# Splitting the score maxima on VectorE, and reading the hidden layer's banks together, in a fused attention block

## The reference, cut to what matters

```python
q = rope(x @ Wq.T + bq) * HEAD_DIM ** -0.5      # 16 heads of 16
k = rope(x @ Wk.T + bk)
v = x @ Wv.T + bv
attn = softmax(q @ k.T)                          # 1024 x 1024 a head
x = layernorm(x + (attn @ v) @ Wo.T + bo)
W1q, W2q = ternary(W1), ternary(W2)              # each weight -1, 0 or 1
h = relu(x @ W1q.T + b1)                         # 1024 hidden features
x = layernorm(x + h @ W2q.T + b2)
```

## Time and profile before

| | |
|---|---|
| median of 3 runs | 3485.83 us (3482.68 to 3487.73) |
| the profiled execution | 3487.73 us, span 3485.9 us |
| mean granted TensorE clock | 0.969 of full |
| PE busy | 3324.2 us, 95% |
| PE weight loads busy | 1817.4 us, 52% |
| DVE busy | 2981.4 us, 86% |
| ACT busy | 2513.1 us, 72% |
| POOL busy | 2110.0 us, 61% |

### The profile page before, as it was taken

The page is one execution under the profiler, slowest core; times in us unless marked ns, Lnnn a source line. Parts: engine busy times, 40 slices in busy tenths (PEclk is TensorE's granted clock), DMA queues, the critical chain, the costliest instruction groups (busy, mean ns, idle before and its releaser), DMA issues.

```text
span 3485.9 us, 80529 instructions
## 1 busy us (share of the span) xinstructions
PE 3324.2 (95%) x30726; PEld 1817.4 (52%) x30726; DVE 2981.4 (86%) x5543; ACT 2513.1 (72%) x4884; POOL 2110.0 (61%) x2281
## 2 busy tenths in 40 slices
PE   4898999999999999999999999999999999999975
PEld 3443455555555555555555555555555555544444
DVE  4777899999999999999999999999999999999611
ACT  2156777777777777777777777777777777777740
POOL 2133576677666766676667666766676667643446
PEclk9589999999999999999999999999999999999987
DMA  5334344544453345344543454345434544444110
GB/s 144 49 81 96 90 96 112 111 101 93 112 119 95 91 112 119 95 93 110 119 100 90 110 118 101 98 103 115 104 100 99 114 102 104 96 91 82 34 41 25
DMA packets 292290, 336.94 MB, mean 97 GB/s; under 512 B 59712, under 2 KB 241856, under 8 KB 291648
## 3 DMA queue, kind: packets, MB, share of 16 engines
q1 hardware_dynamic: 291904, 331.79, 41.4%
HBM read 193.27 MB, written 138.41 MB: 95 GB/s over the span
## 4 chain that ended last, share of the span: by engine, by line
PE 92%; POOL 2%; DVE 2%; ACT 1%; DMA 1%; issue 1%; SPq 0%; POOLq 0%; DVEq 0%; ACTq 0%
PE ob L652 29%; PE sc L635 28%; PE job L507 25%; PE ms L624 9%; DVE mxp L1027 1%; ACT prob L756 1%; POOL hid_r L1100 1%; PE job L560 0%; PE ms L507 0%; POOL ka L1186 0%; PE ob L507 0%; DMA qa<-qk_parts 0%; DMA xt_sb<-xt 0%; DVE mxp L879 0%; DMA maxima<-nm 0%
## 5 line engine op out<-in xcount | busy, mean ns | idle before, releaser
L879 DVE TENSOR_REDUCE mxp<-ms 128x1 f32<-128x512 f32 x4032 | 2602.6, 683 | 276.0 <-PE ms L624 226.6
L756 ACT ACTIVATE prob<-sc 128x512 f32<-128x512 f32 x4096 | 2225.4, 597 | 743.0 <-PE sc L635 717.3
L635 PE MATMUL sc<-qa,ka 50*128 50x512 f32 x4096 | 1556.4, 446 | 41.9 <-ACT prob L756 35.0
L624 PE MATMUL ms<-ka,qa 48*128 48x512 f32 x4032 | 1540.8, 449 | 2.0 <-DVE mxp L879 2.0
L635 PEld LDWEIGHTS sc<-qa,ka 50*128 50x128 f32 x4096 | 688.3, 186 | 1142.5 <-ACT prob L756 1023.6
L652 PE MATMUL ob<-prob,v_sb 128*17 128x512 f32 x8192 | 1087.4, 603 | 0.3
L624 PEld LDWEIGHTS ms<-ka,qa 48*128 48x128 f32 x4032 | 681.4, 186 | 16.6 <-DVE mxp L879 13.9
L1079 POOL TENSOR_TENSOR ve<-mv,eps_sb 128x2 f32<-128x2 f32 x128 | 24.9, 194 | 576.2 <-DVE mv L906 576.2
L1100 POOL TENSOR_TENSOR hid_r<-hid,hid_r 128x512 fp32r<-128x512 f32 x256 | 328.8, 1284 | 20.5
L1068 POOL TENSOR_TENSOR xt_r<-xt_sb,xt_r 128x512 fp32r<-128x512 f32 x64 | 83.3, 1301 | 328.6 <-ACT xt_r L768 302.9
L507 PEld LDWEIGHTS job<-h_t,w_sb 64*128 64x128 f32 x3840 | 261.5, 186 | 22.8
(11 more groups left out here) (101 smaller groups left out, 2768.0 us busy)
## 6 DMA issues: line engine op xcount, KB each, us to landing
qk_parts<-parts SPq DMA_DIRECT2D x128, 512.0 KB, 4.7
ka<-qk_parts SPq DMA_DIRECT2D x384, 128.0 KB, 4.5
qa<-qk_parts SPq DMA_DIRECT2D x384, 128.0 KB, 7.4
attention<-at_st SPq DMA_DIRECT2D x128, 256.0 KB, 2.9
v_ones<-v_st SPq DMA_DIRECT2D x64, 272.0 KB, 3.3
v_sb<-v_ones SPq DMA_DIRECT2D x64, 272.0 KB, 8.7
xt_sb<-xt SPq DMA_DIRECT2D x64, 256.0 KB, 4.8
xn<-x SPq DMA_DIRECT2D x64, 256.0 KB, 4.6
```

The lines of the kernel that those rows point to most:

```text
L624: nc.tensor.matmul(ms[upto(b, g, NS1, at) % MS_BANKS][:, :], operand(qa, b, g, j, ROWS)[:, qt * P:(qt + 1) * P], operand(ka, b, g, j, ROWS ...
L635: nc.tensor.matmul(sc[upto(b, g, HG * STEPS, n) % SC_BANKS][:, :], operand(ka, b, g, j, ROWS + MROWS)[:, tt * P:(tt + 1) * P], operand(qa, ...
L756: nc.scalar.activation(prob[st_ % 2][:, j, :], sc[upto(b, g, HG * STEPS, n) % SC_BANKS][:, :], ACT.Exp).then_inc(s["exp_done"], 1)
L879: nc.vector.reduce_max(mxp[(b * G + g) % 2][:, kh, j * TT + qt:j * TT + qt + 1], ms[upto(b, g, NS1, at) % MS_BANKS][:, :], AX.X).then_inc( ...
```

## The change

There are two parts.

**Maxima.** The table `MAXIMA_AT` gets `turn` in part 1 of step 8 instead of part 2, and two new entries, `high` in part 2 and `low` in part 3. Both are DVE instructions on 128x32 elements: `high` multiplies the transposed maxima by -1 and writes the high part (one input in SBUF), `low` multiplies by -1 and subtracts the high part (two inputs in SBUF). POOL's `split_maxima`, three instructions a unit, is gone, with its tiles `neg` and `zeros` and the semaphore `negated`.

**Hidden tiles.** At `f1` and `f3` ACT takes both tiles of `job[0]` between exponentials 1 and 2, and `finish_rest` is gone. DVE takes both tiles of `job[1]` in part 1, instead of one in part 1 and one in part 2.

```diff
-MAXIMA_AT = {(8, 0): "combine", (8, 2): "turn"}
+MAXIMA_AT = {(8, 0): "combine", (8, 1): "turn", (8, 2): "high", (8, 3): "low"}
...
                 elif name in ("f1", "f3"):
-                    take_hidden(b, g, int(name[1]) - 1, job[0][:, 0:TQ])
-
-            def finish_rest(job_):
-                stage, at, name = job_
-                if name in ("f1", "f3"):
-                    take_hidden(*at, int(name[1]), job[0][:, TQ:2 * TQ])
+                    for p in range(2):
+                        take_hidden(b, g, int(name[1]) - 1 + p, job[0][:, p * TQ:(p + 1) * TQ])
...
                         exps(b, g, st_, 3)
-                        for job_ in jobs_at(b, g, st_, tail):
-                            finish_rest(job_)
...
+                elif part == "high":
+                    dve.wait_ge(s["mx_turned"], upto(b, g, 1, 1))
+                    wait_used(dve, s["m_stored"], upto(b, g, 32, 0))
+                    nc.vector.tensor_scalar(nm[:, 0, :], mxt[:, :], -1.0, None, ALU.mult).then_inc(s["high_done"], 1)
+                elif part == "low":
+                    dve.wait_ge(s["high_done"], upto(b, g, 1, 1))
+                    nc.vector.scalar_tensor_tensor(out=nm[:, 1, :], in0=mxt[:, :], scalar=-1.0, in1=nm[:, 0, :],
+                                                   op0=ALU.mult, op1=ALU.subtract).then_inc(s["mx_taken"], 1)
...
-                            for stage, at, name in jobs_at(b, g, st_, tail):
-                                if stage == "proj" and part == 1:
+                            for stage, at, name in jobs_at(b, g, st_, tail) if part == 1 else []:
+                                if stage == "proj":
                                     take_key_half(*at, name)
-                                elif name in ("f1", "f3") and part in (1, 2):
-                                    p = part - 1
-                                    take_hidden(*at, int(name[1]) - 1 + p, job[1][:, p * TQ:(p + 1) * TQ])
+                                elif name in ("f1", "f3"):
+                                    for p in range(2):
+                                        take_hidden(*at, int(name[1]) - 1 + p, job[1][:, p * TQ:(p + 1) * TQ])
...
-            def split_maxima(b, g):
-
-                pool.wait_ge(s["mx_turned"], upto(b, g, 1, 1))
-                nc.gpsimd.tensor_tensor(neg[:, :], zeros[:, :], mxt[:, :], ALU.subtract).then_inc(s["negated"], 1)
-                pool.wait_ge(s["negated"], upto(b, g, 1, 1))
-                wait_used(pool, s["m_stored"], upto(b, g, 32, 0))
-                nc.gpsimd.tensor_copy(nm[:, 0, :], neg[:, :]).then_inc(s["high_done"], 1)
-                pool.wait_ge(s["high_done"], upto(b, g, 1, 1))
-                nc.gpsimd.tensor_tensor(nm[:, 1, :], neg[:, :], nm[:, 0, :], ALU.subtract).then_inc(s["mx_taken"], 1)
...
-                if not (last and g == G - 1):
-                    split_maxima(b + (g + 1) // G, (g + 1) % G)
...
-            split_maxima(0, 0)
```

More of the change, by code:

```diff
@@ L192, in build @@
         eps_sb = sb("eps_sb", [P, TL])
-        zeros = sb("zeros", [P, HG * TT])
         asum = sb("asum", [P, 2])
@@ L216, in build @@
         mxt = sb("mxt", [P, HG * TT])
-        neg = sb("neg", [P, HG * TT])
         nm = sb("nm", [P, MROWS, HG * TT], fp32r)
@@ L258, in build @@
             rotated parts_done parts_stored v_stored
-            m_stored m_loaded s1_ready s1_taken max_done mx_turned negated high_done mx_taken
+            m_stored m_loaded s1_ready s1_taken max_done mx_turned high_done mx_taken
             s2_ready exp_done pv_done o_taken ob_zero
@@ L1136, in finish_second_norm, with unit @@
                                         ).then_inc(s["res_done"], 1)
-            def unit(b, g, tail, tail_before, last):
+            def unit(b, g, tail, tail_before):
                 proj = projected(b, g)
@@ L1174, in unit, with batch @@
                     normalise(*prepared(b, g))
-            def batch(b, tail=True, tail_before=True, last=False):
+            def batch(b, tail=True, tail_before=True):
                 for g in range(G):
-                    unit(b, g, tail, tail_before, last)
+                    unit(b, g, tail, tail_before)
             nc.gpsimd.memset(half_sb[:, :], -0.5).then_inc(s["powers_set"], 1)
             nc.gpsimd.memset(eps_sb[:, :], EPS).then_inc(s["powers_set"], 1)
-            nc.gpsimd.memset(zeros[:, :], 0.0).then_inc(s["powers_set"], 1)
-            pool.wait_ge(s["powers_set"], 3)
+            pool.wait_ge(s["powers_set"], 2)
             for i in range(2 * RING):
@@ L1200, in _ @@
             batch(B - 2)
-            batch(B - 1, last=True)
+            batch(B - 1)
             finish_second_norm(B - 2, G - 1)
```

## The result

The changed kernel took 3530.85 us (median of 4 runs, 3526.58 to 3533.51); the kernel before took 3485.2 beside it. The ratio is 1.013, interval [1.0112, 1.0147]: 45.6 us slower, where I had forecast 56 (3541). The profiled execution took 3532.56, its span 3530.8.

The account below looks back on a forecast made before the run. The loop closing each step, through ACT's exponentials, and PE's almost equally late matmul stream were taken as the bound. -14.5 + 22 + 50 = +57.5, less 2 for overlap, +56, gave 3541 us; range 3484 to 3578.

Parts of the forecast that it names:

- The start: First two units: inputs issued earlier, ACT's stalls of 5.9 and 5.1 us go, plus 3.5 for PE's clock: -14.5 us.
- Hidden tiles on ACT: Second tile ahead of exponentials 2 and 3 delays the next step's second score: 0.37 us in 60 units, 22 us.
- Maxima on DVE: `high` and `low` wait for POOL: 0.75 in step 9, 0.3 in step 10, minus 0.13; 54 units, 50 us.
- The lock that doesn't bite: Rival: `high` and `low` are short enough to get in between POOL's instructions; sum +7, 3493 us; chance 0.18.
- six: Sign: `low` takes at most 0.3 us in the last six units with a tail, where POOL is idle.
- POOL not let go between its instructions: Rival: `high` too waits for POOL's second instruction, third and fourth pair of step 9 stall; 3575 us; chance 0.11.
- The faster side: Rival: PE has room for the late second score in steps 10 and 12, no lock wait; 3477 us; chance 0.08.
- The start that keeps its stalls: Rival: something else holds the inputs at the start, such as POOL's split parts; 3556 us; chance 0.05.
- ACT's copies: Sign the forecast is right: ACT's input copies at the end of the first two units wait for nothing.

Follow-up runs that it names:

- pool_early: The kernel before with POOL's split of the maxima moved ahead of the second set's rotations, in the first two units alone: 3474.99 us against 3487.91, ratio 0.9965.
- hidden_only: The kernel before with the hidden tiles grouped on both ACT and DVE, the maxima staying on POOL: 3511.45 us against 3487.91, ratio 1.0065.
- hidden_dve_only: The kernel before with the hidden tiles grouped on DVE alone, ACT keeping its order: 3491.61 us against 3487.91, ratio 1.0005.
- act_late: The changed kernel with ACT's order of before (second hidden tile after exponential 3), DVE's tiles still grouped: 3519.13 us against 3489.8, ratio 1.0079.
- after_halves: The changed kernel with each of POOL's four sums cut into two instructions of half the length: 3502.36 us against 3488.26 for the kernel before, ratio 1.004.
- low_zero: The changed kernel with the low part written as zeros by a DVE instruction that reads nothing: 3502.01 us against 3489.8 for the kernel before, ratio 1.0034.

## Why the prediction was right

The direction and the mechanisms were right, the sum 10 us too high.

*The start (-14.5).* Right. The stalls that end are 5.9 in the first unit, 7.2 in the second and 1.4 in the third, slow clock included: 14.5. `pool_early`, which touches only them, gained 12.9 [6.3, 18.1 by its ratio's interval]. The clock in the windows from 200 to 290 us, before and after:

```profile
200.00:290.00 90.00, 76.96 (x602) 35.34 (x598) 64.89 (x109) 58.59 (x114) 42.29 (x36) 0.91 0.40 93
```

```profile
200.00:290.00 90.00, 85.61 (x716) 39.58 (x715) 77.58 (x136) 68.55 (x134) 50.25 (x37) 1.00 0.48 105
```

After a wait of PE it stood at 1.2 GHz before; without these waits it stays at 2.4.

*Hidden tiles on ACT (+22).* Right: `hidden_only` has 0.405 us a unit for my 0.37, 24 us over 60 units, and `hidden_dve_only` shows that nothing of it is DVE's while the maxima stay on POOL.

*Maxima on DVE (+50).* Right in kind, too large in size, and this is the step that was mis-sized: 0.75 + 0.3 - 0.13 = 0.92 a unit, where the changed kernel has 1.131 - 0.405 = 0.73 (39 us). Step 10 came as forecast, 3.40. Step 9 grew by 0.57, not 0.75. I had let `low` begin its own work at POOL's recorded end and so put step 9's first reduction 1.79 into the step; it starts at 1.64 (1708.94), since `low` ends at 1709.01, only 0.05 after line 328's record (1708.96), and not its own length of 0.18 after it. Over 54 units the 0.19 between 0.92 and 0.73 is 10 us, as much as the whole miss. The other terms differ less: with -14.5, +24 and +39 the sum is 49, inside the interval of the result (39 to 51). Step 10's cause I had right too (the third reduction, 0.5 into the step for my 0.6); `act_late` shows that the ACT part isn't added to it there, so to take off 0.13 was right.

*The rivals.* The lock that doesn't bite (3493) is out: `low` takes 0.75 in all 54 units with the sums there and 0.18 to 0.19 in the last five (five, where I had written six: the last unit makes no maxima), and `after_halves` and `low_zero` each bring step 9 back to 3.18. POOL not let go between its instructions (3575) is out: `high` ends at 1707.75, while line 328's record has begun at 1707.66, and a reduction runs behind it. The faster side (3477) is out with `hidden_only`: 0.405 is above its point of 0.24 a unit. The start that keeps its stalls (3556) is out by ACT's copies.

Two inputs aren't needed for the wait. The Trainium skill (SBUF — State Buffer, "SBUF: two separate sides") names instructions with two SBUF inputs and those in a 2-port mode. `high` has one input, and it waits in every steady unit (0.66 us at least); the transpose, also with one input, takes its 0.20 beside POOL. That agrees with the page if `high` runs in such a mode, which no run here shows.

## What to carry to other kernels

A short DVE instruction on SBUF of the kind of `high` or `low` costs what is left of POOL's current instruction, so its price is read from what POOL does at that place, not from its own length. Shorter POOL instructions made it cheap here (`low` 0.19 instead of 0.75). Two changes that are tried alone can hide a cost that they have together: DVE's grouped tiles cost 0.006 us a unit alone and 0.161 behind the maxima. Before a small step is moved from one engine to another, ask which queue it delayed in its old place: here the waits in SP's queue in the first two units were all there was to gain, and reordering it alone gave 0.5%. A read of PSUM placed ahead of two exponentials delays the bank that the next step's second score waits for; here two such reads a unit, 0.37 us each, came out as 0.4 a unit.

## What the hardware showed that I had not expected

- `high` and `low` end 0.03 to 0.05 us after the record of the POOL instruction that they waited for, though alone they take 0.17 to 0.18. So some 0.13 us of them lies ahead of that recorded end; whether DVE is let go early, does part of the work while it waits, or POOL's record runs long isn't shown. `high` gets in between two POOL instructions whose records overlap.
- A one-input instruction on 128x32 elements waits (0.17 us alone, 0.85 beside POOL); a memset of the same size (0.085) and a transpose (0.20) don't.
- The same program's first unit took 71.5 us in one profile and 82.2 in another, its granted clock at 0.50 up to 155 us in the one and 171.5 in the other; PE was busy 52.8 of 82 us in that stretch of the first, and 83.1 of 116.5 of the second:

```profile
73.00:155.00 82.00, 52.78 (x129) 26.90 (x129) 58.32 (x97) 5.16 (x10) 2.49 (x2) 0.50 0.53 81
```

```profile
55.00:171.50 116.50, 83.13 (x287) 44.52 (x287) 80.97 (x131) 15.33 (x31) 11.40 (x9) 0.50 0.41 71
```

What ends such a stretch stays open.
